# Four conditioned transformer blocks on one core: a new order of the steps from layer 0 into layer 1, waits per half, and transfers of negated maxima issued by ScalarE

## What is computed

```python
# each layer, for each of the 4 sequences h [512, 256]
n = norm(h) * (1 + scale(cond)) + shift(cond)        # layer 0: rmsnorm, others: layernorm
q, k, v = n @ Wq, n @ Wk, n @ Wv
# layer 0: one head of 256; layers 1, 2, 3: 16 heads of 16 (layer 1: q and k L2-normalised)
h = h + gate * ((softmax(q @ k.T * scale) @ v) @ Wproj)
m = norm2(h) ...
h = h + gate * (gelu(m @ W1) @ W2)                   # layers 0, 1, 2; hidden size 1024
# layer 3 has a norm with the style in place of the MLP
```

## Time and profile before

| | |
|---|---|
| median of 3 runs | 1216.73 us (1213.23 to 1219.13) |
| the profiled execution | 1216.2 us, span 1214.4 us |
| busy: PE, PEld, DVE, ACT, POOL | 93%, 59%, 58%, 66%, 40% |
| mean granted TensorE clock | 0.955 of full |
| layer 0 with the lead-in of job 4, up to the first score of window 4 | 0 to 259.82 us |
| windows 4 to 7 (layer 1) | 259.82 to 577.56 us |
| windows 8 to 11 (layer 2) | 577.56 to 914.96 us |
| windows 12 to 15 (layer 3) and the end | 914.96 to 1214.40 us |

### The profile page before, as it was taken

How to read it: one execution, slowest core, us unless ns; L and a number is a source line. 1 busy time by engine, 2 the same in 40 slices (tenths; PEclk the granted TensorE clock), 3 DMA queues, 4 the chain that set the end, 5 groups by cost and what they waited for, 6 DMA issues and landing times.

```text
span 1214.4 us, 19892 instructions
## 1 busy us (share of the span) xinstructions
PE 1126.0 (93%) x6676; PEld 716.0 (59%) x6676; DVE 702.9 (58%) x1448; ACT 802.1 (66%) x1436; POOL 488.1 (40%) x443
## 2 busy tenths in 40 slices
PE   7889999798799999999999999999999999998986
PEld 5577878674255665657556556666566475454433
DVE  6545362746165155334865855857747648778673
ACT  2563735458587778786677686686775766666563
POOL 1453555260344425453354353253443342434032
PEclk8899999899798999999999999999999999889797
DMA  6010000052613303330242232133203312333301
GB/s 223 17 36 18 1 1 18 5 88 39 146 45 62 80 1 79 80 50 20 46 90 62 65 71 48 25 70 71 42 22 53 62 21 56 75 58 62 71 8 38
DMA packets 40997, 64.49 MB, mean 53 GB/s; under 512 B 11816, under 2 KB 26920, under 8 KB 40896
## 3 DMA queue, kind: packets, MB, share of 16 engines
q1 hardware_dynamic: 40896, 63.21, 25.1%
HBM read 22.90 MB, written 2.12 MB: 21 GB/s over the span
## 4 chain that ended last, share of the span: by engine, by line
PE 62%; ACT 11%; DVE 10%; issue 8%; SPq 5%; POOL 2%; DMA 2%; ACTq 0%; POOLq 0%; DVEq 0%
PE ring L565 12%; PE ring L566 11%; PE ring L567 11%; PE AVB L668 9%; PE ring L655 8%; ACT probs L845 4%; SPq L518 4%; PE ring L632 4%; DVE m L1155 3%; PE ring L688 2%; DVE stats L1013 1%; PE ring L605 1%; ACT L845 1%; ACT gT_h L913 1%; PE ring L693 1%
## 5 line engine op out<-in xcount | busy, mean ns | idle before, releaser
L845 ACT ACTIVATE probs<-ring 128x512 f32<-128x512 f32 x768 | 399.8, 620 | 135.3 <-PE ring L632 83.6
L1155 DVE TENSOR_REDUCE m<-ring 128x1 f32<-128x512 f32 x512 | 318.8, 682 | 129.5 <-PE ring L632 120.3
L655 PE MATMUL ring<-SQ,SK 49*128 49x512 f32 x768 | 242.6, 456 | 19.7 <-ACT probs L845 12.4
L655 PEld LDWEIGHTS ring<-SQ,SK 49*128 49x128 f32 x768 | 115.8, 195 | 160.5 <-issue 79.2
L632 PE MATMUL ring<-SK,SQ 48*128 48x512 f32 x512 | 202.5, 467 | 6.3 <-ACT probs L845 2.2
L668 PE MATMUL AVB<-probs,V 128*32 128x512 f32 x1536 | 203.6, 642 | 0.6 <-issue 0.5
L1256 POOL TENSOR_TENSOR gT_l<-gT_f,gT_h 128x512 fp32r<-128x512 f32 x96 | 121.2, 1284 | 61.9 <-ACT gT_h L913 59.7
L632 PEld LDWEIGHTS ring<-SK,SQ 48*128 48x128 f32 x512 | 88.2, 191 | 41.9 <-ACT probs L845 28.0
L565 PE MATMUL ring<-w_h,gT_h 128*128 128x256 f32 x384 | 109.8, 286 | 0.8 <-POOL gT_l L1256 0.7
L566 PE MATMUL ring<-w_l,gT_h 128*128 128x256 f32 x384 | 106.7, 278 | 0.0
L567 PE MATMUL ring<-w_h,gT_l 128*128 128x256 f32 x384 | 106.6, 278 | 0.0
(11 more groups left out here) (180 smaller groups left out, 2129.1 us busy)
## 6 DMA issues: line engine op xcount, KB each, us to landing
SQ<-qh SPq DMA_DIRECT2D x192, 64.0 KB, 2.3
SK<-kh SPq DMA_DIRECT2D x192, 64.0 KB, 2.3
SQ<-ql SPq DMA_DIRECT2D x96, 64.0 KB, 2.3
SK<-kl SPq DMA_DIRECT2D x96, 64.0 KB, 2.3
raw<-in_w SPq DMA_DIRECT2D x20, 256.0 KB, 2.8
wmod_s<-in_wmod SPq DMA_DIRECT2D x6, 512.0 KB, 4.0
gates<-gate_rows SPq DMA_DIRECT2D x12, 256.0 KB, 3.5
raw<-in_wqkv SPq DMA_DIRECT2D x9, 256.0 KB, 2.9
```

The costliest lines, as they stand in the source:

```text
L655: mm = pe.matmul(o[:, :], SK[a % 4][r:r + KS + 1, n // 2, c * P:(c + 1) * P], SQ[a % 4][r:r + KS + 1, n // 2, :], start=True, stop=True)
L845: act.activation(probs[:, n % PROBS, :], bank(kind, a, i)[:, :], ACT.Exp, scale=SCALE[layer(unit_job(a))]).then_inc(done["scores"], 1)
L1155: nc.vector.tensor_reduce(m16[:, 80 * (a % 2) + col:80 * (a % 2) + col + 1], bank(kind, a, i)[:, :], AX_X, ALU.max, negate=True).then_inc( ...
```

## The change

Five things change. The tables get new numbers, with tables of their own for each job of layer 0 (`SINGLE0` to `SINGLE3`, `FFN1`), and the patterns of pairs change at some places. The MLP of job 3 gets due times of 23.3 to 31.85 ticks in place of 7.93 to 17.25, that is, inside window 4. PE waits for the halves of `hT1`, `hT2`, `oT2` and `av0` one by one, and some other waits of ACT are for the step that truly was the last reader (`POST_READ`, `split_qkv`); q and k have a semaphore each. Five matmuls that compute nothing (`WARM_Q`) stand ahead of the first `q`. The two transfers of a unit's maxima are issued by ACT, after its exponential of score 13 of the unit before.

```diff
-SINGLE3 = {"stat1": (-21.91,), "norm1": (-19.26,), "hT1": (-9.4, -9.24), "q": (-6.86, -3.56), "k": (-6.6, -3.6),
-FFN3 = {"hT2": (7.93, 9.27), "fc1": (9.97, 10.12, 10.26, 10.41, 14.34, 14.49, 14.64, 14.79), "gelu": (10.56, 14.93),
+FFN3 = {"hT2": (23.3, 23.61), "fc1": (25.85, 25.86, 25.87, 25.88, 29.8, 29.81, 29.82, 29.83), "gelu": (25.89, 29.84),
...
-WARM = 12
+WARM, WARM_Q = 12, 5
...
+POST_READ, _reader = {}, None
+for _s in PLAN:
+    if _s[0] in ("hT2", "oT2", "av0") and _s[2] == 0:
+        POST_READ[_s] = _reader
+    if _s[0] in ("proj", "fc1"):
+        _reader = _s
...
-                elif kind == "shift":
-
-                    sp.wait_ge(done["shift"], nth("shift", a))
-                    for par in range(2):
...
-                        sp.dma_start(dst, s.bitcast(F32)).then_inc(shifted[a % 4], 16)
...
+                if (kind, a, i) == ("q", 0, 0):
+                    for _ in range(WARM_Q):
+                        pe.matmul(o[:, :], SK[0][:, 0, 0:P], SK[0][:, 0, :], start=True, stop=True)
                 if kind in ("q", "k", "qktok", "v"):
-                    pe.wait_ge(done["hT1"], nth("hT1", a, CH - 1))
+                    pe.wait_ge(done["hT1"], nth("hT1", a, 0))
...
                         for c in range(CH):
+                            pe.wait_ge(done["hT1"], nth("hT1", a, c))
                             mm = product(o[:, :], [w[:, c, off:off + P] for w in (wqkv_h, wqkv_l)],
                                          [h[:, c, :] for h in (hT_h, hT_l)], c == 0, c == CH - 1)
...
                 elif kind == "fc1":
-                    pe.wait_ge(done["hT2"], nth("hT2", a, CH - 1))
                     pe.wait_ge(done["split_w1"], nth("split_w1", layer(a), i // 2))
                     for c in range(CH):
+                        pe.wait_ge(done["hT2"], nth("hT2", a, c))
...
                     act.activation(probs[:, n % PROBS, :], bank(kind, a, i)[:, :], ACT.Exp,
                                    scale=SCALE[layer(unit_job(a))]).then_inc(done["scores"], 1)
+                    u = a + 1
+                    if i == 13 and u < UNITS * JOBS and not bounded(unit_job(u)):
+
+                        act.wait_ge(done["shift"], nth("shift", u))
+                        slot_free(act, u)
+                        for par in range(2):
+                            d = SQ[u % 4][BLK * par + KS:BLK * par + KS + 1, :, :]
+                            dst = bass.AP(d.tensor, d.offset, [[2 * TOK, 1], [P, 8], [1, P]]).bitcast(F32)
+                            r = 32 * (u % 2) + 8 * par
+                            act.dma_start(dst, cT[r:r + 8, :].bitcast(F32)).then_inc(shifted[u % 4], 16)
```

More of the change, by code:

```diff
@@ L69 @@
[L69 to L73, removed]
[3 rows of a table removed]
[L77 to L86, removed]
@@ L92 @@
-QKV = {"hT1": (-19.4, -15.49), "q": (-13.4, -12.45), "k": (-13.2, -10.05), "v": (-8.75, -4.6),
-       "stack": (-8.75, -7.25, -1.55, 0.85), "stat1": (-22.85,), "norm1": (-21.55,)}
-ATTN = {"oT1": (17.05, 17.51, 17.52, 17.53), "oT2": (18.15, 18.61), "proj": (19.25, 19.9), "stat2": (21.0,),
+          "shift1": (-3.9,), "crow": (-3.65, -3.05, -1.05, 0.95)}
+QKV = {"hT1": (-19.2, -15.64), "q": (-13.25, -12.6), "k": (-12.75, -10.05), "v": (-8.75, -4.85),
+       "stack": (-8.25, -6.15, -1.05, 1.45), "stat1": (-22.45,), "norm1": (-21.55,)}
@@ L95 @@
+ATTN = {"oT1": (17.05, 17.51, 17.52, 17.53), "oT2": (18.5, 18.66), "proj": (19.15, 19.8), "stat2": (21.0,),
         "norm2": (22.5,)}
-FFN = {"hT2": (23.6, 23.91), "fc1": (25.55, 25.56, 25.57, 25.58, 29.5, 29.51, 29.52, 29.53), "gelu": (25.59, 29.54),
-       "fc2a": (27.7, 29.5), "fc2": (30.8, 31.35)}
-FFN3 = {"hT2": (7.93, 9.27), "fc1": (9.97, 10.12, 10.26, 10.41, 14.34, 14.49, 14.64, 14.79), "gelu": (10.56, 14.93),
-        "fc2a": (12.38, 13.26), "fc2": (16.8, 17.25)}
-OUTPUT = {"gatefix": (18.95,), "final": (24.6, 26.4, 26.45, 30.8), "store": (24.55, 26.85, 29.05, 32.4), "bias": (18.05,)}
@@ new lines @@
+FFN3 = {"hT2": (23.3, 23.61), "fc1": (25.85, 25.86, 25.87, 25.88, 29.8, 29.81, 29.82, 29.83), "gelu": (25.89, 29.84),
+        "fc2a": (27.45, 29.2), "fc2": (31.65, 31.85)}
+OUTPUT = {"gatefix": (21.15,), "final": (25.2, 25.4, 26.45, 30.15), "store": (26.5, 28.85, 29.05, 32.7), "bias": (18.5,)}
+LAST = {"bias": (-0.75,), "gatefix": (17.7,), "oT1": (16.0, 16.01, 16.02, 16.03), "oT2": (16.65, 16.96),
+        "proj": (17.8, 19.3), "base": (19.3, 26.3), "stat2": (21.35,), "centre": (21.5, 21.6, 21.7, 23.1),
+        "final": (23.2, 25.15, 26.9, 29.7), "store": (21.15, 22.9, 23.2, 23.3)}
@@ L123, in timed @@
+FFN1 = {"hT2": (17.27, 17.62), "fc1": (20.82, 21.18, 21.53, 21.59, 25.14, 25.5, 26.58, 27.63), "gelu": (21.94, 27.99),
+        "fc2a": (25.87, 26.52), "fc2": (34.6, 34.78)}
+START = [("stat1", 0, 0), ("load_mod", 0, 0), ("load_qkv", 0, 1), ("load_qkv", 0, 0), ("load_qkv", 0, 2),
+         ("load_w1", 0, 2), ("load_wp", 0, 0), ("load_mod", 0, 1), ("modrow", 0, 0), ("load_w1", 0, 0),
[3 rows of a table added]
 def timed(table, j):
@@ L714, in _ @@
                         for c in range(CH):
+                            if c > 0 and a < JOBS - 1:
+                                pe.wait_ge(done["oT2" if multi(a) else "av0"], nth("oT2" if multi(a) else "av0", a, c))
                             src = [h[:, c, tok:tok + P] for h in (postT_h, postT_l)]
@@ L884, in _ @@
                     act.wait_ge(pe_ring, use(kind, a, i))
-                    if i == 0 and layer(a - 1) < LAYERS - 1:
-                        act.wait_ge(pe_ring, use("fc1", a - 1, MT - 1))
-                    elif i == 0:
-                        act.wait_ge(pe_ring, use("proj", a - 1, 1))
+                    if i == 0:
+                        act.wait_ge(pe_ring, use(*POST_READ[(kind, a, i)]))
                     if a == JOBS - 1:
```

109 lines of the change are left out of this document (63 added, 46 removed), and 12 rows, old and new, of tables (FIRST, START).

## The result

The median of 4 runs is 1243.6 us (1234.0 to 1245.1). On the same chip the kernel before took 1216.3 us (4 runs, 1213.2 to 1219.1): a ratio of 1.021, with a 95% interval of 1.015 to 1.027. The profiled execution took 1245.1 us, the slowest of the four.

A forecast was written before the change was run, and what follows sets the result against it. PE bounds layer 2, DVE's maxima pace layer 3, and window 4 has room. Terms of -2 - 24.8 + 11.5 - 1 + 3 + 25 = +11.7 on 1216.2 give 1228 us, range 1203 to 1249.

The forecast's parts named there:

- The start, -2: Kernel start: five matmuls hidden in the `hT_l` wait, waits per half and a steadier clock give -2 us (0 to -4).
- Stages before window 4, -24.8: Ahead of window 4: 17.4 us of moved work, 6.4 of waits and 1 for halves leave; between -14 and -30.
- step (b): Lead-in: two `av0` of job 3 fill PE's wait for `qknorm`; of 8.65 us, 2.2 stay, 6.4 gained.
- Window 4, +11.5: First window of layer 1 takes in 17.4 us of moved work and grows to 79 us; between +7 and +20.
- Rival 2: Window 4 pays full price: stages ahead gain 20, window 4 pays 20, with +28 the total is 1242 us; chance 0.13.
- Rest of layer 1, -1: Windows 5 to 7: waits per half and small moves give -1 us, between -4 and +4.
- Layer 2, +3: ScalarE's wait for DVE's copy and its issue cost about 1 us at one unit in four: +3, between 0 and +9.
- Layer 3, +25: Nothing hides the late landing of ScalarE's transfers in layer 3: +25 us, between +10 and +40.
- The nine boundaries, 9 x 2.3 = 20.7: Units 50, 51, 52, 54, 55, 56, 58, 60 and 62 each lose 2.3 us to the late transfer.
- The clock, +3: Layer 3: nine new PE waits cost some clock, +3 us; by the Trainium skill's rule it would be nearer 10.
- rival 1: Layer 3 hides the landing, with DVE and ACT winning back nearly all of a stall: 1208 us; chance 0.22.
- Rival 4: ACT's issues wait for SP's stack issues at six units of layer 3: 7 us more, 1235 us; chance 0.07.

The follow-up runs named there:

- run 11: The changed kernel with SP issuing the transfers, and PE again waiting for both halves of hT1, hT2, oT2 and av0: 1204.1 us, ratio 0.990.
- order_only: Also called run 2: the changed kernel, but SP issues the transfers at the place of `shift` as before: 1197.1 us, ratio 0.984.
- run 5: order_only, with SP waiting for exponential 12 of the unit before ahead of its issue: 1218.6 us, ratio 1.004.
- run 9: order_only, with SP waiting for exponential 13 of the unit before at nine units of layer 3: 1227.4 us, ratio 1.009.
- issue_only: The kernel before, with only the two transfers issued by ScalarE after exponential 13: 1262.4 us, ratio 1.038.
- run 10: The changed kernel, with SP issuing the transfers at units 49, 53, 57 and 61 alone: 1223.2 us, ratio 1.007.
- run 6: order_only, with two more transfers that nobody reads issued by ScalarE behind exponential 13, without waiting: 1198.7 us, ratio 0.986.
- run 12: order_only with one `stack` number changed, so one unit in four's q and k transfers stand behind the maxima's on SP: 1202.3 us, ratio 0.989.
- run 4: order_only, with the tables of the kernel before from window 8 on (layers 2 and 3): 1206.1 us, ratio 0.992.
- run 3: The changed kernel, but ScalarE issues at the place of `shift` in the list, not after exponential 13: 1216.5 us, ratio 1.000.
- run 7: order_only, with two spare transfers issued by ScalarE behind exponential 13, after waiting for DVE's copy (`shift`): 1207.2 us, ratio 0.994.

## Why the prediction was wrong in size

The sign was right, and so was the mechanism of the largest loss, the late landing. The time lies in the range, but outside the forecast's own 1221 to 1236: 28.9 us slower in the profiled execution, where 11.7 were forecast. Of the 17.2 us between them 6.9 are in layers 0 and 1, 3.3 in layer 2 and 7.0 in layer 3. By its steps, on 1216.2 us:

- **The start, -2**: measured -3.3 (23.05 us against 26.36), clock 1.00 in place of 0.87. With the waits for both halves again (run 11) it takes 25.57 us, with order_only 23.32, so most of it is the halves. What the five matmuls and the changed waits of ACT did, no run shows apart.
- **Stages before window 4, -24.8**: measured -20.2. The wait for `qknorm` went from 5.57 to 0.63 us, as step (b) said. The sum there had an error: it counted the wait of 3.08 us inside the chain from 223.29 on, but that wait had ended at 222.93. It went as well, so the two waits fell by 8.0 us, not 6.4. What the step did not name is a new wait in the same stage, behind `gmax`:

```profile
225.72 3.05 DVE L1164 TENSOR_REDUCE m<-ring 128x4 f32<-128x512 f32 x5
...
228.92 0.39 PE L660 MATMUL ring<-ident,m 128*64 128x128 f32 x1 [4.83 <-DVE m L1164]
```

  PE's `shift1` waits for DVE, which has eight instructions of norm statistics (1.8 us of the 4.83) between the maxima. The work left the path of one DVE chain and met the next.
- **Window 4, +11.5**: measured +14.1 (81.63), within its bounds of +7 to +20. Rival 2, which names nearly the measured total, came true in one half: the stages ahead gained 20.2, but window 4 paid 14, not 20, and layers 2 and 3 paid 38.3, not 28.
- **Rest of layer 1, -1**: measured 0.0 (-3.6, +3.7, -0.1). Together layers 0 and 1 gave 9.4 where 16.3 were predicted. Of the halves, put at 1 us and part of the start, run 11 shows 7, give or take 4.
- **Layer 2, +3**: measured +6.3, but most of it need not be the issue. Order_only, where SP issues, has +5.3 here, runs 5, 9 and 11, also with SP, have +0.9 to +4.7; issue_only, with the old order, has +7.9. So the new order and ScalarE's issue each cost something, and the profiles do not divide it. What the issue does is seen: it waits for the copy at units 34, 38, 42 and 46, and exponential 15 ends at +5.1 there in place of +2.6.
- **Layer 3, +25**: measured +32.0. The order, put at nothing here, gained 6.9 us of it (292.61 against 299.46), so the late issue cost 38.9 (run 2), not 25. This is the step that went wrong most, in one sentence of it above all: "Units 53, 57 and 61 have projections in between and lose nothing". I asked there only whether the transfer lands in time, and it does. I did not ask what is queued behind ScalarE's wait for the copy: `postT_h`, for which DVE and then PE wait. I had asked it for layer 2. Against order_only the first scores of units 49, 53, 57 and 61 come 13.9 us later in sum, and run 10 puts the price of the four at 14 to 17 us. The sign that the prediction named shows it too: window 14, with unit 57 in it, was to be 4 us longer and is 9.2 (75.71 against 66.51); window 13 was to be 7 and is 5.8.
- **The nine boundaries, 9 x 2.3 = 20.7**: against before, the nine first scores come 22.7 us later in sum, so the size is near. Unit 59, which the prediction held apart, is 1.4 us earlier than before, as it said (1 us). Unit 63, put at 2 us, pays nothing: it waits for 1.97 us before and after, and for an exponential, not for the transfer. At unit 58 the issue began 0.46 us earlier than assumed (in the exponential, not behind it), and the landing took longer: 3.07 us from first issue to score (1126.28 to 1129.35) in place of 2.67. The two errors cancel, which was luck: score 0 at +3.67, predicted +3.76. DVE stood for 1.76 us, predicted 2.2.
- **The clock, +3**: in windows 12 to 15 PE is busy 8 us longer than before (269.6 against 261.9) and 11 longer than in order_only. The term was for the late landings alone, and for these it is near: from window 12 to the end PE is busy for 267.1 us in order_only, 270.0 with the late landings but not the four units (run 10), 272.5 with SP's late landings (run 9) and 277.7 in the change. So 3 to 5 us belong to the landings and nearly 8 to the four units that were to lose nothing. Runs 6, 11 and 12, close to order_only, have 262.7 to 264.1, so a few us of this are chance. The Trainium skill's rule, "TensorE: Matmul & The Clock Gate", section "HAM oscillation — how this bites in real kernels", by which the term would have been nearer 10, has the direction right (the clock in window 14 is 0.86, before 0.92); that its size was the better guide for these waits is not shown.
- **The small moves of layers 2 and 3**, costed at nothing, gained some 9 us (run 4). Without them the change would be slower still, so a gain that was not foreseen hides part of the loss.

Of the other rivals: rival 1 (hidden landing) falls by ten waits of 2.7 us. Rival 3 falls with the size of the loss. Rival 4 falls by the issues themselves: 30 of ScalarE's 64 issues ran while SP issued too, with a median of 0.627 us and at most 0.705; the other 34 have the same median, and the longest of all (1.246 us) stood alone. In run 3 one issue beside SP's did take 1.40 us, so it can happen, but not at the price of 6 x 1.2 us.

The accounts of ScalarE's issue, 46 us: late landing 30, give or take 5 (run 9); wait for the copy 10, give or take 3 (run 7); issues that fit beside an exponential 2, give or take 4 (run 6). Their sum of 42 does not differ from 46 by more than these margins. Run 10 prices the issue at four units of layer 3 at 17, give or take 8, which run 7 with its shorter issues need not reach. What the longer issue of the real transfers costs by itself is not shown, since no run had real issues without their landing.

## What to carry to other kernels

Before a transfer is given to another engine, take its issue time from three things: when its data is ready, when that engine's queue gets there, and what stands behind it in the queue while it waits. The last cost 3.4 us at each of four units here, as much as a late landing did at each of nine (30 us in run 9). A transfer that takes about 3 us from issue to use must be issued that far ahead: issued late by SP it cost 30 us too (run 9), and issued earlier by ScalarE it won 26 us (run 3). One place in a list is not right for two stages: price each stage apart, and a gain in one (19 us here) is best taken without the part that loses.

## What the runs showed of the hardware

- A DMA issue on ScalarE starts while its activation is still running: 1126.28 against an exponential from 1126.21 to 1126.81. A pair of 0.62 us vanished beside an exponential (run 6); the pair of 1.28 us left it idle for 0.85.
- The length of an issue differs with the transfer: 0.31 us for eight rows of a constant tile into a plain block of DRAM (run 6), 0.63 to 0.64 for the same amount into strided places of the query stack. Which of the differences between the two makes it was not tried.
- From first issue to the score that needs both transfers it is 3.00 to 3.10 us at the ten late units when ScalarE issues, and 2.56 to 2.67 when SP does (at unit 58 of run 9, 1111.06 to 1113.62), with pairs of the same length. What makes the half microsecond was not tried.
- Issues of ScalarE and SP at the same time were not longer than apart: median 0.627 us for the 30 that overlapped and for the 34 that did not.
- Behind a wait of PE of 1.53 us at unit 57 some of the next products ran at the lower clock level: the granted clock from score 13 to score 0 was 0.87, and the same 59 matmuls took 1.88 us longer than in run 10, where it was 1.00. Units 49 and 53 show the same, and so does run 3. In run 7, where PE waited there for 0.9 us, the clock stayed at 1.00.
